# A third pair of score banks in an attention loop, and transposes of x issued in runs of eight

## The reference

```python
def _L0_attn_ref(x, w_qkv, w_proj, b_proj):          # 16 heads of 64, 8 groups
    qkv = grouped_linear(x, w_qkv, None)              # (8,128,384): block-diagonal
    qkv = jnp.transpose(qkv.reshape(B, N, 3, H, D), (2, 0, 3, 1, 4))
    q, k, v = (qkv[0] * scale, qkv[1], qkv[2])
    attn = jax.nn.softmax(jnp.einsum('bhnd,bhmd->bhnm', q, k), axis=-1)
    out = jnp.einsum('bhnm,bhmd->bhnd', attn, v)
    out = jnp.transpose(out, (0, 2, 1, 3)).reshape(B, N, C)
    return grouped_linear(out, w_proj, b_proj)
def _bitlinear(x, w):                                 # int8-like rows, ternary weights
    return jnp.einsum('bsi,oi->bso', _act_quant(x), _weight_quant(w))
def _L0_ffn_ref(x, w_gate, w_up, w_down):             # inner 4096
    gate = jax.nn.silu(_bitlinear(x, w_gate))
    return _bitlinear(gate * _bitlinear(x, w_up), w_down)
x = _layernorm(x + _L0_attn_ref(x, ...))
x = _layernorm(x + _L0_ffn_ref(x, ...))
```

## Time and profile before

| | |
|---|---|
| Median of 3 runs | 2177.12 us (2177.03 to 2183.22) |
| The profiled execution's own time | 2178.28 us |
| Its span on core 3 | 2176.3 us (the cores: 2158.6 to 2176.3) |
| Load of x, until Q, K, V begin | 120 us |
| First exp to the last phase's projection | 197 to 1156 us |
| FFN, gate and up from | 1224.7 us |
| Busy over the span: PE, DVE, ACT | 62%, 42%, 45% |
| Mean granted TensorE clock | 0.849 |

### The profile page before, as it was taken

One profiled execution on the slowest core, in us unless ns is written; L12 is line 12 of the kernel. 1 busy time (PEld: TensorE's weight loads), 2 busy tenths in 40 slices (PEclk: granted clock), 3 DMA queues, 4 the chain that ended last, 5 costly groups with the idle time before them and its releaser, 6 DMA issues.

```text
span 2176.3 us, 20607 instructions; the slowest of 8 cores (2158.6 to 2176.3 us)
## 1 busy us (share of the span) xinstructions
PE 1351.5 (62%) x5502; PEld 464.5 (21%) x5502; DVE 924.7 (42%) x1742; ACT 970.6 (45%) x1079; POOL 45.0 (2%) x84
## 2 busy tenths in 40 slices
PE   0067666566656665056663599954999737676582
PEld 0011111111111111011111244411444313232231
DVE  1148740453558334385516544444444441203023
ACT  1177877488856877048871121155211461001011
POOL 0000000000000000001000000000000000000000
PEclk9999888688878888568885799976999868898896
DMA  7789940134752788745811543334344415676772
GB/s 192 218 252 321 311 155 1 39 90 127 201 135 78 185 202 233 214 110 170 222 44 49 133 76 78 78 115 117 63 95 95 116 83 165 154 208 180 179 207 82
DMA packets 371458, 314.02 MB, mean 144 GB/s; under 512 B 296593, under 2 KB 298641, under 8 KB 369298
## 3 DMA queue, kind: packets, MB, share of 16 engines
q1 hardware_dynamic: 339712, 234.97, 43.0%
q10 hardware_dynamic: 23186, 48.38, 6.6%
q0 software_dynamic: 8448, 29.37, 3.6%
HBM read 161.49 MB, written 83.89 MB: 113 GB/s over the span
## 4 chain that ended last, share of the span: by engine, by line
PE 36%; ACT 22%; DMA 14%; DVE 12%; issue 7%; SPq 7%; ACTq 2%; DVEq 1%; POOL 0%; POOLq 0%
PE ps L84 36%; ACT A L84 22%; DVE A L84 8%; SPq L84 7%; DMA A<-wg 3%; DMA wdt_sb<-wdqT_s 2%; DVE ln_sb L84 2%; ACTq L84 2%; DMA wtstage<-wdq_s 2%; DMA A<-wqkv 2%; DMA A<-wproj 1%; DMA xre_f<-xp_s 1%; DVE h L84 1%; DMA A<-wu 1%; DMA wdqT_s<-wtstage 1%
## 5 line engine op out<-in xcount | busy, mean ns | idle before, releaser
L84 ACT ACTIVATE A<-ps,cst_sb 128x1024 bf16<-128x1024 f32 (+1 forms) x544 | 575.2, 1087 | 274.8 <-DVE A L84 144.6
L84 PE MATMUL ps<-A,A 128*65 128x512 bf16 (+1 forms) x2048 | 529.8, 429 | 268.8 <-ACT A L84 258.7
L84 PE MATMUL ps<-wg_sl,xqT 128*128 128x512 bf16 x1024 | 266.5, 407 | 114.4 <-DVE h L84 101.3
L84 PE MATMUL ps<-wdt_sb,hqT 128*128 128x512 bf16 x1024 | 246.3, 402 | 110.5 <-DMA wdt_sb<-wdqT_s 52.2
L84 PEld LDWEIGHTS ps<-A,A 128*65 128x65 bf16 (+1 forms) x2048 | 125.0, 105 | 671.7 <-issue 671.7
L84 ACT ACTIVATE A<-ps,scg 128x512 f32<-128x512 f32 x128 | 87.9, 687 | 331.8 <-PE ps L84 309.8
L84 DVE SCALAR_TENSOR_TENSOR h<-ps,scu,A 128x512 bf16<-128x512 f32 x128 | 96.1, 751 | 217.6 <-ACT A L84 213.3
L84 DVE TENSOR_SCALAR A<-A,wsc 128x1024 f32<-128x1024 f32 x96 | 72.3, 753 | 212.8 <-DMA A<-wg 101.5
L84 DVE TENSOR_SCALAR A<-A 128x1024 f32<-128x1024 f32 (+1 forms) x208 | 144.4, 694 | 33.2 <-DVE A L84 17.5
L84 PEld LDWEIGHTS ps<-wg_sl,xqT 128*128 128x128 bf16 x1024 | 104.0, 103 | 253.1 <-issue 146.8
L84 PEld LDWEIGHTS ps<-wdt_sb,hqT 128*128 128x128 bf16 x1024 | 102.1, 102 | 254.6 <-issue 153.8
(11 more groups left out here) (66 smaller groups left out, 704.0 us busy)
## 6 DMA issues: line engine op xcount, KB each, us to landing
A<-wg SPq DMA_DIRECT2D x64, 512.0 KB, 6.4
A<-wu SPq DMA_DIRECT2D x64, 512.0 KB, 5.9
A<-wd SPq DMA_DIRECT2D x64, 512.0 KB, 6.1
wdt_sb<-wdqT_s SPq DMA_DIRECT2D x128, 256.0 KB, 3.3
hq_s<-h ACTq DMA_DIRECT2D x16, 1024.0 KB, 3.9
A<-x SPq DMA_DIRECT2D x16, 512.0 KB, 5.7
xt_s<-A POOLq DMA_DIRECT2D x16, 512.0 KB, 4.4
A<-xt_s ACTq DMA_DIRECT2D x16, 512.0 KB, 3.4
```

The source lines that it names most:

```text
L84: ins = getattr(eng, meth)(*args, **kw)
```

## The change

The attention gets a third pair of score banks: step kc uses banks 0 and 1, 2 and 3, or 6 and 7, by kc modulo 3. TensorE issues three ST pairs ahead of the first PV, and ST(k+3) behind PV(k). A7 keeps its two halves. Since banks 6 and 7 also serve the three sums of `emit_wsum` and half of the projection's products, waits are added: both of these now wait for the exps issued so far (`c_exp`), and an ST into bank 6 waits for the scales (`c_wsc`) and for the projection's additions (`c_radd`).

Apart from that, the list `_xt_q` is gone: the eight transposes of a chunk are issued together, behind the loads of row tiles 4, 8, 12 and 15.

```diff
     _chunk_at = {}
-    _xt_q = []
...
         for k2 in _chunk_at.get(i, []):
-            for g in range(8):
-                _xt_q.append((k2, g))
-        for _ in range(3 if i < T - 1 else len(_xt_q)):
-            if not _xt_q:
-                break
-            k2, g = _xt_q.pop(0)
             need = min(T, 4 * (k2 + 1))
             wait("sync", "s_xbf0", 16 * ((need + 1) // 2))
             wait("sync", "s_xbf1", 16 * (need // 2))
             r0, r1 = k2 * 512, min(N, k2 * 512 + 512)
-            if k2:
-                wait("sync", f"s_xt{g}", 16 * k2)
-            dma("sync", A1[:, g * 2048 + r0: g * 2048 + r1],
-                xbf_s[r0:r1, g * 128:(g + 1) * 128], f"s_xt{g}",
-                transpose=True)
+            for g in range(8):
+                if k2:
+                    wait("sync", f"s_xt{g}", 16 * k2)
+                dma("sync", A1[:, g * 2048 + r0: g * 2048 + r1],
+                    xbf_s[r0:r1, g * 128:(g + 1) * 128], f"s_xt{g}",
+                    transpose=True)
...
     def emit_wsum():
         wait("tensor", "c_bpb", 1)
+        wait("tensor", "c_exp", c("c_exp"))
         wait("tensor", "c_wma", c("c_wma"))
...
             def emit_st(kc):
-                par = kc % 2
-                wait("tensor", "c_exp", base_exp + kc - 1)
-                em("tensor", "matmul", bank(par * 2),
+                b3 = (0, 2, 6)[kc % 3]
+                wait("tensor", "c_exp", base_exp + kc - 2)
+                if b3 == 6:
+                    wait("tensor", "c_wsc", c("c_wsc"))
+                    wait("tensor", "c_radd", c("c_radd"))
+                em("tensor", "matmul", bank(b3),
...
-                em("tensor", "matmul", bank(par * 2 + 1),
+                em("tensor", "matmul", bank(b3 + 1),
...
             emit_st(0)
             emit_st(1)
+            emit_st(2)
             for kc in range(T):
                 par = kc % 2
+                sb3 = (0, 1024, 3072)[kc % 3]
...
-                   ps[:, par * 1024:(par + 1) * 1024], AF.Exp, bias=cst[:, 0:1],
+                   ps[:, sb3:sb3 + 1024], AF.Exp, bias=cst[:, 0:1],
...
-                if kc + 2 < T:
-                    emit_st(kc + 2)
+                if kc + 3 < T:
+                    emit_st(kc + 3)
...
             wait("tensor", "c_rcp", c("c_rcp"))
+            wait("tensor", "c_exp", c("c_exp"))
             base_radd = c("c_radd")
```

## The result

| | before | changed |
|---|---|---|
| Median | 2180.73 us, 8 runs (2177.03 to 2185.01) | 2130.75 us, 8 runs (2126.79 to 2134.89) |
| Profiled execution: time | 2178.28 us | 2133.07 us |
| Profiled execution: span of the slowest core | 2176.3 us, core 3 | 2130.0 us, core 4 |
| All cores | 2158.6 to 2176.3 us | 2113.6 to 2130.0 us |

The changed kernel takes 0.9772 of the time before, interval 0.9757 to 0.9787: about 50 us less. In some executions of these kernels the cores of one die show a lower granted clock and the time can be some per cent longer; the ratios and intervals leave the clearly longer executions out, the medians keep them. 2136 was predicted, with 2112 to 2160 as the range. The profiled executions differ by less, 2178.28 - 2133.07 = 45.2 us, and the predicted sum of -41.4 is to be compared with that.

What follows compares the result with a forecast made beforehand. ScalarE's exps, held up by waits for TensorE, were taken to set the attention's pace. 24 blocks at 1.85 us (-44.4) and +3 at the start made -41.4 from 2178.28; median forecast 2136 us, range 2112 to 2160.

Steps and rivals of the forecast that it cites:

- What an exp waits for: Attention blocks: exps stop waiting for an ST queued behind PV; at full clock 1.01 us per exp against 1.165.
- 1.85 us per block: Attention blocks of phases 0, 1 and 3: each of 24 blocks gets 1.85 us shorter, 44.4 us in all.
- At the half clock only the pair that is ahead is won: Start of a block: TensorE's 1.53 us step stays the bound, so only the pair now ahead wins, 0.5 us.
- Phase 2 doesn't pay: Attention phase 2: VectorE's quantization units bound it, so its blocks' gain becomes longer waiting; 14.8 us not counted.
- Phase 1 is just covered: End of attention phase 1: five blocks win 9.3 us, within VectorE's 11.07 us of idle time.
- The start: Before the first exp: x transposes in runs of eight delay loads of x; +3 us, range -0.5 to +8.
- The waits added cost nothing: Waits on c_exp, c_wsc and c_radd: nothing; without cover by exps 0 and 1, c_radd costs 1 us per phase.
- ScalarE's wait for PE: Sign, over all 512 exps: ScalarE's wait for TensorE falls from 81.1 to some 30 us.
- The PV wait in the ST's place: Rival, chance 0.15: in attention blocks released exps don't overlap, steps are 1.11 us, 26 us come back, 2162.
- The clock's drop vanishes: Rival, chance 0.05: at block boundaries the half clock disappears, blocks take 3.6 us less, time 2101.
- The half clock holds for whole blocks: Rival, chance 0.03: attention exps stay at 1.53 us, blocks take 3.4 us more, time 2262.
- TensorE's step grows: Rival, chance 0.02: in attention TensorE's full-clock step rises a quarter to 1.25 us, 22 us slower, 2202.

Runs made afterwards that it cites:

- the kernel before with the fill: Kernel before (two score-bank pairs), second ST pair repeated twenty times at each block's start but a phase's first, output unchanged: 2144.89 us, ratio 0.9873.
- the fill: Changed kernel, third ST pair repeated twenty times in TensorE's idle gap at each block's start but a phase's first, output unchanged: 2107.67 us, ratio 0.9680.
- ten repeats: Changed kernel, third ST pair repeated ten times more at each block's start but a phase's first, output unchanged: 2124.39 us, ratio 0.9759.

## Why the prediction was right, step by step

- **What an exp waits for.** Right. The gap of 0.20 us ahead of every second exp came from ST(k+2) standing behind PV(k), and with ST(k+3) there the exps run eleven in a piece. Fixing the clock instead leaves the gap in place (the kernel before with the fill, 0.21 and 0.32 us).
- **1.85 us per block.** Right in size: 14.4, 15.7 and 15.1 us in phases 0, 1 and 3 are 1.80, 1.96 and 1.89 per block. Its working for block 14 held to a tenth for exps 2 and 3 (2.50 and 4.03 after the first; 2.56 and 4.09 forecast) and exp 4 (5.57; 5.5), and was short at the end: the half clock lasted one exp longer, and the last exp started at 17.15, not 16.6. So block 14 won 1.45 us, not 2.0. That the average still came out is partly luck. The prediction took the average below its 2.0 because a longer block would win less; the traces show the reverse. From first to last start of a block's exps the mean over all cores and the blocks of phases 0, 1 and 3 fell from 18.98 to 16.90 us. Block 14 was one of the short blocks before (18.60), and those of 19.0 and more won about 2.3, those below 18.8 about 1.7. Two errors of opposite sign met.
- **"At the half clock only the pair that is ahead is won."** Right for the change as it is: the working has exps 2 and 3 wait for PV(0) and PV(1) at TensorE's pace, and they did. What it missed is that this wait can be taken away with profit, as the run with a third part of A7 did, which won some 12 us by letting ScalarE go on. Behind the miss, and behind the wrong expectation of that run, stands a bound that was read too high: "ST at most 0.46" in the earlier trace rows held a wait for the exp. Unhindered it is 0.32, so the full-clock step is 0.87 and does not "just fit" beside an exp of 1.01; TensorE can catch up.
- **Phase 2 doesn't pay.** Right as a mechanism: the units and the transposes are its bound, and spreading them frees 71 us. Mis-sized: 0 was written, -4.0 measured, also -4.1 with the banks in phase 2 alone.
- **Phase 1 is just covered.** Covered, with more room than forecast: 5.61 us of idle time on core 4 and 1.69 on core 3, where 1 to 3 was forecast. So the end was nearer on some cores: on cores 2 and 3 the reciprocal came 11 us behind the start of the last exp instead of 7.9, since the turned sums landed later, and their phase 1 took 194.1 us against 190.7 to 192.6 on the others. In the second execution of the changed kernel one core's reciprocal (core 0) had no idle time at all and its phase 1 took 196.4 us, so the cover doesn't hold on every core. What delayed the sums was not followed.
- **The start.** +3 was forecast with -0.5 to +8. The profiled execution has +5.3 between its two slowest cores and +2.7 between the medians, and the second execution of the changed kernel +0.2; the transposes alone cost 1 to 7 us. That is within the range, and not much more can be said of the size.
- **The waits added cost nothing.** The projections stayed at 24.2 to 24.3 us, and no new wait stands ahead of an exp but those named.
- **ScalarE's wait for PE.** 47.6 us, not some 30. 30 us is 0.9 per block, less than the working for block 14 gives by itself (0.44 + 0.42 + some 0.3 for exps 2 to 4); measured are 1.5 (1.64 in block 14, four gaps).
- **The rivals.** *The PV wait in the ST's place*: no steps of 1.11, a piece of eleven has ten overlaps; fallen. *The clock's drop vanishes*: the gap fell only from 5.44 to 5.18 and the drop stayed; the fill shows that the drop can be had away, and its price in phases 0 and 3 is 11 to 12.6 us each. The rival's 3.6 us a block doesn't follow from its own numbers: 25.6 less 15.2 + 6.5 is 3.9, and a block with banks and fill takes 21.6. *The half clock holds for whole blocks*: fallen; 0.93 over the 13 us from 566. *TensorE's step grows*: not in the profiled execution. But it has to be corrected. In the profiled execution of the banks alone, cores 4 to 7 had a mean granted clock of 0.811 to 0.814 and the others 0.844 to 0.847. On core 7, busy time in a block and in the gate and up stage (columns as in the earlier trace rows), and the weight loads in that block:

```profile
566.00:578.00 12.00, 11.67 (x46) 2.73 (x44) 7.01 (x10) 11.75 (x12) 0.00 (x0) 0.80 0.75 194
1280.00:1330.00 50.00, 50.00 (x233) 22.67 (x232) 23.49 (x45) 9.62 (x14) 0.00 (x0) 1.00 0.36 73
```

```profile
572.25 0.15 PEld L84 LDWEIGHTS ps<-A,A 128*65 128x65 bf16 x2 [0.28 <-issue]
572.90 0.10 PEld L84 LDWEIGHTS ps<-A,A 64*128 64x128 bf16 x2 [0.50 <-issue]
573.27 0.15 PEld L84 LDWEIGHTS ps<-A,A 128*65 128x65 bf16 x2 [0.27 <-issue]
```

A step is 0.65 + 0.37 = 1.02 us there, at a granted clock of 0.80. The last eleven exps of that block take 11.34 us in one piece where 11.16 stands above, so it costs 0.02 a step, and the spans of the two dies differ by 5 us in the medians (2114.7 and 2119.4). The rival's 1.25 came from a quarter on top of 1.01; the quarter has to go on the unhindered 0.87. The Trainium skill ("TensorE: Matmul & The Clock Gate", section "Seeing it yourself", the warning on the peak-current limiter) has a limiter that takes a whole die to 13/16 = 0.81 of the clock. These four cores agree with that figure, and so do cores 0 to 3 in the profiled execution of the kernel with the third part of A7 (means of 0.806 to 0.815). The prediction said that the trace does not agree; for the kernel before and the gate and up stage that holds (1.00 with PE busy 50.00 of 50.00 us), for the attention it does not always. What brings the lower clock on was not found: core 7 has 0.80 in the attention and 1.00 in the denser stage of the same execution.

## What to carry to other kernels

When a wait is taken away, name the next one at each level of the clock, and take the slower engine's step from a place where nothing holds it; a step read where it waits is too long, and hides that the engine can catch up. Count the gain only in the stages that the freed engine bounds, and look at who is late at each stage's end: here moving the side work of one phase (0.977 to 0.947 of the time before, some 65 us) was worth more than the whole change. A short idle gap of TensorE ahead of a dense loop is worth filling, but by these runs only if the fill reaches nearly to its end: ten repeats left 3.05 us idle and won little, twenty left 0.92 and won about 1%. Where a longer wait lies ahead of the fill, it runs at the lower clock and delays what it was to help. And hold a forecast that was worked out on one block against many blocks before its working is called right.

## What the runs showed of the hardware that was not expected

- Exps that follow without a gap start 1.00 to 1.02 us apart at 1.11 us each, in pieces of 11 (11.16 us) and of 16 (16.45 us): each overlaps its forerunner by 0.09 to 0.11, though each has a wait ahead of it, which was met in time.
- TensorE idle for 5.18 us came back to a granted clock of 0.53 over the next 6 us (block 14 of the changed kernel), idle for 3.05 us to 0.50 (core 3, with ten repeats). Idle for 0.92 us between twenty repeats and the first PV it had 1.00 throughout, and 16 exps without a gap.
- In the profiled execution of the banks alone, a core of one die has a granted clock of 0.80 in an attention block and 1.00 in a stage where TensorE is busy throughout.
- A chain of loads, VectorE operations and stores that no exp is waited on in (phase 2's units) ran 2 to 5 us shorter of 288 when the blocks beside it were shorter. The cause is open.
